# Gate pass of a graph network: adjacency product ahead of the node look-up, rank counts read one step sooner, edge places worked out one step later

## The reference

```python
gate = jax.nn.silu(edge_attr @ F1W + F1b) @ F2W + F2b
ei = emb[atom_z[src]]
ej = emb[atom_z[dst]]
gate = gate + (ei * (ej @ adapt)).sum(-1, keepdims=True)
cw = jnp.where(distances < CUT, 0.5 * (jnp.cos(jnp.pi * distances / CUT) + 1.0), 0.0)
mj = node_mult[dst]
msg = gate * h[dst] * (cw * mj)[:, None]
agg = jax.ops.segment_sum(msg, src, num_segments=N)
tot = jnp.clip(jax.ops.segment_sum(mj, src, num_segments=N), 1e-08, None)
```

## Time and profile before

| | us |
|---|---|
| time before, median of 3 runs | 9959.81 (9945.05 to 9967.33) |
| the profiled execution, its own time | 9949.76 |
| its span in the trace | 9947.9 |
| the gate pass in the trace | from about 2893 to about 4877 |

### The profile page before, as it was taken

The page is one execution under the profiler, slowest core; times in us unless marked ns, Lnnn a source line. Parts: engine busy times, 40 slices in busy tenths (PEclk is TensorE's granted clock), DMA queues, the critical chain, the costliest instruction groups (busy, mean ns, idle before and its releaser), DMA issues. The chain is left out here.

```text
span 9947.9 us, 371312 instructions
## 1 busy us (share of the span) xinstructions
PE 7979.0 (80%) x155927; PEld 7386.4 (74%) x155927; DVE 6211.9 (62%) x15995; ACT 5112.6 (51%) x15184; POOL 6234.8 (63%) x7484
## 2 busy tenths in 40 slices
PE   6566666666548888888689987999799969997999
PEld 6455555555537777777579987998699969996999
DVE  6455555555547777777767767776677767775111
ACT  0122222222137777777567775777477757773000
POOL 0477777777736666666467765777477747773000
PEclk9677777777669999999789988999799969997999
DMA  8412212121125555545267745676377627763665
GB/s 352 168 43 48 48 43 48 43 48 43 38 84 181 179 176 174 173 172 182 95 189 217 215 149 157 211 215 187 112 216 220 210 89 214 213 213 144 251 250 211
DMA packets 1080220, 1546.28 MB, mean 155 GB/s; under 512 B 152061, under 2 KB 1001125, under 8 KB 1061404
## 3 DMA queue, kind: packets, MB, share of 16 engines
q1 hardware_dynamic: 976147, 1446.12, 43.6%
q0 software_dynamic: 102400, 76.26, 3.8%
HBM read 1102.83 MB, written 417.48 MB: 153 GB/s over the span
## 5 line engine op out<-in xcount | busy, mean ns | idle before, releaser
L773 POOL DMA_INDIRECT edge_records<-rec_out,slot_i x1600 | 1931.4, 1207 | 821.6 <-issue 821.6
L1778 ACT ACTIVATE vals<-carry_h,weight 128x49 f32<-128x49 f32 x9604 | 2320.3, 326 | 6.4
L1615 PE MATMUL psum<-TT,hd_t 128*128 128x97 bf16 x28812 | 1532.8, 209 | 146.3 <-DMA hs_t<-one_hots 105.3
L1615 PEld LDWEIGHTS psum<-TT,hd_t 128*128 128x128 fp8e4 x28812 | 1370.5, 99 | 166.2 <-issue 163.1
L1823 POOL TENSOR_TENSOR vals<-vals 128x343 f32<-128x343 f32 x1372 | 1042.0, 759 | 92.9
L716 ACT COPY one_bsT<-psum 49x500 f32<-49x500 f32 x400 | 207.9, 568 | 1656.3 <-PE psum L699 1656.3
L1818 POOL TENSOR_TENSOR vals<-vals 128x343 f32<-128x343 f32 x1372 | 1042.2, 760 | 4.7 <-ACT vals L1778 4.7
L695 PE MATMUL psum<-ident,key 125*125 125x125 bf16 x1600 | 354.3, 309 | 831.6 <-DVE base L747 773.0
L1618 PE MATMUL psum<-ts,hs_t 128*128 128x49 bf16 x28812 | 983.7, 185 | 42.4 <-issue 41.7
L1683 DVE SCALAR_TENSOR_TENSOR xks<-recs,psum 128x343 f32<-128x343 f32 x1372 | 696.9, 508 | 488.6 <-PE psum L1618 485.8
L695 PEld LDWEIGHTS psum<-ident,key 125*125 125x125 bf16 x1600 | 323.3, 217 | 859.2 <-issue 859.2
(11 more groups left out here) (338 smaller groups left out, 17866.5 us busy)
## 6 DMA issues: line engine op xcount, KB each, us to landing
AJ<-adjacency SPq DMA_DIRECT2D x35, 5488.0 KB, 16.7
recs<-attributes SPq DMA_DIRECT2D x196, 686.0 KB, 5.8
hs<-one_hots SPq DMA_DIRECT2D x392, 336.0 KB, 3.3
one_hots<-hots SPq DMA_DIRECT2D x343, 336.0 KB, 8.0
edge_records<-HA SPq DMA_DIRECT2D x49, 2278.5 KB, 48.9
recs_g<-edge_records SPq DMA_DIRECT2D x49, 2278.5 KB, 9.9
recs<-attributes SPq DMA_DIRECT2D x196, 514.5 KB, 3.8
hd_t<-one_hots SPq DMA_DIRECT2D x196, 448.0 KB, 4.8
```

What stands on the lines that cost most here:

```text
L773: e.indirect_dma_start(REC[:, :], bass.IndirectOffsetOnAxis(ap=slot_i[:, i % 4, s:s + 1], axis=0), rec_out[:, (i // 2) % 4, s, i % 2, :], ...
L1615: e.matmul(D(g, c), hd_t[:, p, g, c, :], TD[:, k, g * GC + c, :], start=k == 0, stop=k == 2)
L1778: last = e.activation(vals[:, c, 0, :], carry_h[:, par(back), c, :], ACT.Copy, scale=weight[:, par(back), c:c + 1])
```

## The change

Two lists are written in another order, and one function is cut in two. On TensorE `make_adj` stands ahead of `look_up_nodes` in each step. On VectorE `take_ranks` goes from lag 4 at the head of step 3 to lag 3 at the end of step 2, and keeps only `DEG` and `counted`; the three instructions on places become `fill_slots` (lines 1349 to 1351 in the changed file), at the end of step 3, behind `make_hot_dst`.

```diff
-                    stages([(1, flip_src), (3, rank), (2, make_same), (1, flip_dst), (5, scatter_group), (2, look_up_kinds), (3, look_up_nodes), (1, make_adj)])
+                    stages([(1, flip_src), (3, rank), (2, make_same), (1, flip_dst), (5, scatter_group), (2, look_up_kinds), (1, make_adj), (3, look_up_nodes)])
...
                             e.tensor_scalar(counted[:, :], bank(6)[:, NB:3 * NB], 1.0, None, ALU.add).then_inc(ranks_taken.sem, 1)
+
+                    def fill_slots(k):
+                        if of(k) == NG - 1:
                             until_row(ranks_taken, k)
                             of_row(slots_stored, 16, back=2)
...
-                    stages([(6, add_row), (4, take_ranks), (4, make_values), (3, pair_up), (0, make_hot_src), (4, second), (0, make_hot_dst)])
+                    stages([(6, add_row), (4, make_values), (3, pair_up), (0, make_hot_src), (4, second), (0, make_hot_dst), (4, fill_slots), (3, take_ranks)])
```

## The result

The changed kernel is slower: 9986.01 us median (9970.56 to 9995.47, 10 runs) against 9961.65 us (10 runs). The ratio is **1.0024, 95% interval 1.0014 to 1.0034**, so some 24 us lost, where 9961 and no change was forecast. The time lies 2 us above the stated range. The ratios leave out one of the twelve runs of e3, which took 12631 us at a granted clock of 0.68 instead of 0.87.

What follows compares the result with a forecast made beforehand. The prediction took a VectorE and GpSimd loop of 5.30 us a step, plus 37.3 us of late steps, as the bound. Its terms, 13.7 + 4 - 18.7 + 2 = +1.0 us, gave 9961 us, no change, range 9938 to 9984.

Steps and rivals of the forecast that it cites:

- The bound: Gate pass: a closed loop of VectorE and GpSimd, 5.30 us a step, plus 37.3 us of steps with late `rest`.
- Part 1, the ranks: VectorE's `take_ranks`: same spot in the queue, so TensorE's 56.3 us wait for `counted` stays, off the loop; gain 0.
- Part 2, the places: VectorE behind `make_hot_dst`: L1349 pays 0.63 us for the read port; 0.28 us a row, 13.7 us lost.
- Rival A: VectorE keeps the read port when L1349 follows at once: 17.2 us gained instead of 13.7 lost, 9930; chance 0.06.
- issued first: Reading of the SBUF port rule: GpSimd's waiting instruction gets the port before VectorE's next, costing 0.63 us.
- Part 2, step 3: End of step 3: earlier `make_values` uses up the 1.4 us cover of `first`, so `rest` is late; 4 us lost.
- Part 3: TensorE, adjacency product ahead of node look-up: a longer lead cuts late steps from 37.3 to 18.6 us; 18.7 gained.
- The slack of 1.8 us: Between the end of `first` and the start of `rest`: 0.5 us now, 1.8 us with TensorE's larger lead.
- the sentence on the nodes: Node look-up 0.39 us later in its step, but `make_values` takes it one step on, over a microsecond to spare.
- the same 15 stand-stills: TensorE's stretches over 1.8 us with only "issue" as cause, between 2925 and 4830: 43.1 us together, 16.1 beyond 1.8 each.
- Part 4, SP's queue: SP waits some 17 us a row for the places; records' load stays hidden, denser transfers cost 2 us, ends 0 and 20.
- Rival C: SP's queue: denser burst of transfers more than doubles TensorE's stand-stills beyond 1.8 us, 18.6 to 41; 9981; chance 0.16.

Runs made afterwards that it cites:

- e3: Changed kernel with the store of a row's places issued one row later, behind the stores of group 3: 9967.63 us, ratio to before 1.0005.
- e10: Changed kernel with `DEG` and `counted` moved behind `make_hot_src` of step 2, into VectorE's idle time; SP's queue unchanged: ratio to before 0.9980.
- e8: Changed kernel with the three places instructions moved behind the product of pairs of step 4, `pair_up` cut in two: ratio to before 1.0001.
- e2: Changed kernel with TensorE's old list (node look-up ahead of adjacency product): 9990.18 us, ratio to before 1.0028.
- e1: Kernel before with only TensorE's new list (adjacency product ahead of node look-up): 9970.42 us, ratio to before 1.0006.
- e5: e3 with `DEG` and `counted` moved behind `make_hot_src` of step 2, into VectorE's idle time: ratio to before 0.9959.
- e4: e1 with SP's queue reordered: stores of groups 0 and 1, next records' load, other stores, previous row's places behind group 3: 9947.0 us, ratio 0.9983.
- e6: Kernel before with only SP's queue changed, to that of e4; both engine lists as before: ratio to before 0.9976.
- e7: Kernel before with e4's SP queue, TensorE's new list, `DEG` and `counted` in step 2's idle time, places behind step 3's product of pairs: ratio 0.9925.
- e9: e7 with TensorE's old list (node look-up ahead of adjacency product): 9882 us median, ratio to before 0.9917.

## Why the prediction was wrong, point by point

**The bound.** Right. VectorE and GpSimd's loop of 5.30 us sets the pace, and the difference inside the pass is found in it.

**Part 1, the ranks, "Gain: 0".** Right as to where the instructions stand: they are at the same spot and TensorE's wait stayed. "That wait was off the loop anyway" was wrong for the changed kernel. The wait grew from 56.3 to 73.7 us, since TensorE came earlier, and more often than before the clock was low behind it (17 rows instead of 6). e10 ends the wait, and gains 30 us beyond the 14 of the instructions that it takes out of the loop.

**Part 2, the places, 13.7 us lost.** Right to the hundredth in each step: L1349 at 1.18 us, 0.29 and 1.67 between starts, 1.96 in all. The reading that GpSimd's waiting instruction goes ahead of VectorE's next one is borne out by 48 of 49 rows here (in the last, L1349 has no `make_hot_dst` ahead of it and takes 0.56 us), and e8 shows the price by taking it away. Rival A is out. The rule that the prediction takes from the Trainium skill ("SBUF — State Buffer", on the two separate sides), read as "issued first", agrees with the 1.18 us.

**Part 2, step 3, "taken 4 us", ends 0 and 6.** The mechanism was right, the size not: **10.7 us**, beyond the end. The slack was put together from an undisturbed row at full clock; its undisturbed share is 0.06 us a row (3 us), nearly all the rest comes in the 17 rows in which `make_same` ran at the lower clock behind the wait for `counted`. It is 3.8 us in e2, where that wait is short, and 20.7 in e3, where it is longest. The window 3510 to 3512 of the kernel after shows such a stretch, with TensorE busy throughout, no transfers, and the clock at its lower level:

```profile
3510.00:3512.00 2.00, 2.00 (x55) 2.00 (x53) 0.82 (x2) 1.41 (x3) 1.36 (x3) 0.50 0.00 0
```

**Part 3, 18.7 us gained.** The late starts of `second` outside step 3 fell from 35.7 to 17.4 us: 18.3. That this is so near to 18.7 is luck. With the order on TensorE alone (e1) they fell by 3.5 us only; in the changed kernel nearly the same sum, 17.2, came up as late starts of `make_values`. The slack of 1.8 us did not come either: its median is 0.71 us before, 1.25 in e1 and 0.91 in the kernel after, and it comes near 1.9 only where the wait for `counted` is taken away or the burst is moved (1.72 in e10, 1.90 in e3 and e5). And nothing was gained on balance, for the sentence on the nodes failed: "`make_values` takes them one step on, with over a microsecond to spare". That holds in an undisturbed step. In a disturbed one the node look-up is now what ends last, as in the rows at 3537: from its end to the start of `make_values` nine of ten groups had over 0.87 us in the kernel before, and now one of ten has 0.1 us or less. It cost **17.2 us** that had no term in the sum. I had counted the same 15 stand-stills against `first` alone and never against the instruction that I was moving to the back. This is the step that failed first of all, and that made a forecast of no change into a loss.

**Part 4, SP's queue, "2 us ... ends 0 and 20".** SP waits 18.4 us a row for the places (881.1 in 48), as forecast at some 17, and no one waited for records. Its cost was mis-sized and is no term of its own: when e3 lets the transfers start early, 16.2 us of late `make_values` go, where 2 were taken, near the lower of the two ends. Rival C named the place and the direction, though not the consumer: TensorE's stand-stills grew from 87 to 108 us, but what exceeds 1.8 us in each of them fell, from 16.1 to 5.9, where C wanted it doubled. e2 (85, with the burst as late as in after) and e1 (109, with the burst as before) show that the growth comes with the order on TensorE. The later burst moves them to later steps.

The measured sum for 47 rows: 13.2 (port) + 10.7 (step 3) + 17.2 (`make_values`) - 18.3 (`second`) = 22.8, against 23.7 in the pass and 24 in the medians.

**The stand-stills.** That TensorE waits in them for its instructions was inferred from "issue". The records of single DMA packets in the kept traces bear it out. In the 48 rows of the kernel before, the queue that the page of the profile calls "q8 instruction" moves 326 packets of 16384 bytes, one for every 256 of TensorE's 83550 instructions there. All 62 stand-stills end 1.15 to 1.65 us behind the end of such a packet, and in the kernel after 79 of 80 do; of moments drawn at random 10% do. In the longest, at 3437, the packet began 1.67 us after TensorE had stopped, took 1.05 us, and TensorE went on 1.35 us later, 4.06 us together. Of the 87 us, 77 lie where the DMA share is above 0.8, which holds for 34% of these rows.

**Left open.** Why the packets of instructions begin so late there; why the stand-stills fall from 47 to 20 us between e3 and e5, where only the wait for `counted` goes; and why the new order on TensorE raises them from 87 to 109 in e1.

## What to carry to other kernels

When an engine is given a lead, look for the next thing that it will wait for: here the lead ran into a semaphore once a row and became a wait of up to 2 us, with the lower clock behind it in many rows. Move the few instructions that end such a wait into time in which their engine idles anyway; that paid 44 us here for 0.29 us of work a row (e10), where the new order on TensorE paid nothing (e1 against before, e4 against e6, e7 against e9). When a product is moved behind another, hold every disturbance in the trace against its new position too, not only against the one that was in the way.

## What the runs showed of the hardware

A wait of TensorE of 2.0 us in a stream that is otherwise busy was followed by a stretch at the lower clock (groups of `make_same` at up to 0.95 us, most of them at just that, instead of 0.55) in 29 of 48 rows of e3, 23 of e1 and 19 of e4. Behind the wait of the kernel after, 1.5 us on average, it came in 17 rows, behind that of the kernel before, 1.2 on average, in 6, and behind that of e2, 0.9 on average, in 3. With the wait gone it came in none of those places (e5, e7, e9, e10).

A GpSimd instruction that waits for a VectorE instruction with two SBUF inputs goes ahead of VectorE's next such instruction even when that one follows at once: 1.18 us instead of 0.55 in the 48 rows of the kernel after in which the two meet. Placed 0.84 us later (e8) it takes 0.56 us.

The order in which SP issues the same transfers, with no byte changed, brought TensorE's stand-stills from 87 to 53 us (e6).

TensorE can stand still for its own instructions, up to 4.06 us at a time: its stand-stills end 1.15 to 1.65 us behind the end of a packet of instructions, in 62 of 62 cases of the kernel before.
